# One-hot compares of 512 columns in place of 256 in a recommendation tower on one core

## What is computed

```
e = stack([tbl_f[ids[:, f]] for f in range(32)], axis=1)   # 2048 x 32 x 128
z = einsum('bfd,bgd->bfg', e, e)[:, iu, ju]                # 496 pairs f < g
h = concatenate([z, dense_ctx], axis=1)                    # 2048 x 512
h = maximum(h @ W_top1 + b_top1, 0)                        # 512 -> 512
h = maximum(h @ W_top2 + b_top2, 0)                        # 512 -> 256
y = h @ W_top3                                             # 256 -> 1
```

## Time and profile before

| | us |
|---|---|
| median of the runs | 439.18 |
| runs | 438.72, 439.18, 439.19 |
| the profiled execution's own time | 440.8 |
| its span, first to last instruction | 438.9 |
| TensorE (PE) busy | 396.6 |
| VectorE (DVE) busy | 337.4 |
| GpSimd (POOL) busy | 307.6 |
| ScalarE (ACT) busy | 121.7 |

### The profile page before, as it was taken

The page is one execution under the profiler, slowest core; times in us unless marked ns, Lnnn a source line. Parts: engine busy times, 40 slices in busy tenths (PEclk is TensorE's granted clock), DMA queues, the critical chain, the costliest instruction groups (busy, mean ns, idle before and its releaser), DMA issues.

```text
span 438.9 us, 11697 instructions
## 1 busy us (share of the span) xinstructions
PE 396.6 (90%) x4672; PEld 371.2 (85%) x4672; DVE 337.4 (77%) x873; ACT 121.7 (28%) x220; POOL 307.6 (70%) x324
## 2 busy tenths in 40 slices
PE   0469677999999999999999999999999999999967
PEld 0468577989999889989999989999999999998866
DVE  3789949999498958899498949899589949891510
ACT  1254410133213321233113321233214311332323
POOL 5777877777777777777777777777777777777100
PEclk9998998899999999999999999999999999999999
DMA  6999953435234332424332442436332543332000
GB/s 131 235 240 215 218 174 80 104 78 100 77 83 77 99 98 57 99 75 103 74 81 72 106 93 58 97 79 100 73 86 72 102 93 66 89 74 54 21 3 2
DMA packets 31374, 42.11 MB, mean 96 GB/s; under 512 B 11164, under 2 KB 24220, under 8 KB 31352
## 3 DMA queue, kind: packets, MB, share of 16 engines
q1 hardware_dynamic: 18936, 20.64, 22.7%
q0 software_dynamic: 10240, 20.99, 18.9%
q10 hardware_dynamic: 2176, 0.17, 0.4%
HBM read 41.77 MB, written 0.01 MB: 95 GB/s over the span
## 4 chain that ended last, share of the span: by engine, by line
PE 55%; DVE 28%; issue 6%; DMA 5%; SPq 3%; ACT 1%; DVEq 0%; ACTq 0%
PE sel_ps L295 19%; DVE onehot L628 17%; PE gram_ps L314 12%; PE work_ps L352 11%; DVE pairs L639 9%; PE work_ps L360 6%; DMA pairs<-tables_selected 5%; PE work_ps L277 3%; PE work_ps L425 2%; SPq L227 1%; SPq L222 1%; DVE table_lo L662 1%; PE work_ps L434 1%; PE work_ps L331 1%; DVE pairs L653 1%
## 5 line engine op out<-in xcount | busy, mean ns | idle before, releaser
L248 POOL DMA_INDIRECT gathered<-table,tile_ids x320 | 307.4, 960 | 100.3 <-issue 95.4
L628 DVE TENSOR_SCALAR onehot<-id_rows,row_no 128x256 fp32r<-128x256 int32 x768 | 238.8, 386 | 19.4 <-DMA id_rows<-ids_selected 12.2
L295 PE MATMUL sel_ps<-onehot,table_hi 125*128 125x256 f32 x768 | 202.0, 300 | 30.1 <-DVE table_lo L662 23.1
L295 PE MATMUL sel_ps<-onehot,table_lo 125*128 125x256 f32 x768 | 194.5, 290 | 0.0
L295 PEld LDWEIGHTS sel_ps<-onehot,table_hi 125*128 125x128 f32 x768 | 152.1, 198 | 38.8 <-DVE table_lo L662 24.0
L295 PEld LDWEIGHTS sel_ps<-onehot,table_lo 125*128 125x128 f32 x768 | 152.7, 199 | 0.0
L639 DVE STREAM_TRANSPOSE pairs<-gram_ps 32x1024 f32<-32x1024 f32 x60 | 74.8, 1246 | 56.0 <-PE gram_ps L314 55.3
L487 ACT ACTIVATE rows_T<-sel_ps 128x512 f32<-128x512 f32 x48 | 30.0, 627 | 127.3 <-PE sel_ps L295 91.9
L314 PEld LDWEIGHTS gram_ps<-rows_T 128*64 128x64 f32 x1920 | 57.5, 138 | 7.2 <-issue 7.2
L478 ACT ACTIVATE rows_T<-work_ps 128x512 f32<-128x512 f32 x80 | 45.5, 599 | 61.1 <-PE work_ps L277 61.1
L314 PE MATMUL gram_ps<-rows_T 128*64 128x64 f32 x1920 | 59.6, 223 | 2.4 <-issue 2.4
(11 more groups left out here) (26 smaller groups left out, 84.1 us busy)
## 6 DMA issues: line engine op xcount, KB each, us to landing
id_rows<-ids_selected SPq DMA_DIRECT2D x48, 256.0 KB
gathered<-table,tile_ids POOLq DMA_INDIRECT x320
pairs<-tables_selected SPq DMA_DIRECT2D x6, 448.0 KB
x<-tables_selected SPq DMA_DIRECT2D x6, 448.0 KB
w_sb<-w SPq DMA_DIRECT2D x1, 1024.0 KB
w_sb<-w SPq DMA_DIRECT2D x1, 512.0 KB
pairs<-tables_selected SPq DMA_DIRECT2D x6, 52.0 KB
x<-tables_selected SPq DMA_DIRECT2D x6, 52.0 KB
```

What stands on the lines that cost most here:

```text
L248: nc.gpsimd.indirect_dma_start(gathered[:, t, g, :], None, tables_gathered[g], bass.IndirectOffsetOnAxis(ap=slot_id, axis=0)).then_inc(chu ...
L295: last_op = nc.tensor.matmul(sel_ps[:, u % 2, e, :], part[0:SEL_P, 2 * u + e, k, :], onehot[0:SEL_P, (2 * u + h) % HALF_SLOTS, kk, e, :], ...
L628: last_op = nc.vector.tensor_scalar(onehot[:, (2 * u + h) % HALF_SLOTS, kk, e, :], id_rows[:, slot, e, :], row_no[:, k:k + 1], None, ALU.i ...
```

## The change

From the second pair on one compare makes the one-hots of both features of a unit for one k: 512 columns in place of twice 256. The two features stand side by side in `id_rows` and in `onehot`, so both operands are 512 consecutive elements. The first pair (`known_first`) keeps its compares of 256. Which values are written, the semaphores, the slots and the order of everything else stay.

```diff
--- before.py
+++ after.py
@@ -624,10 +624,16 @@
                         dve.wait_ge(onehot_used, at(i, o, 2 * UNITS, 2 * u + h - HALF_SLOTS + 1))
                     for kk in range(K_HALF):
                         k = h * K_HALF + kk
-                        for e in range(2):
-                            last_op = nc.vector.tensor_scalar(onehot[:, (2 * u + h) % HALF_SLOTS, kk, e, :],
-                                                              id_rows[:, slot, e, :], row_no[:, k:k + 1], None,
-                                                              ALU.is_equal)
+                        hot = onehot[:, (2 * u + h) % HALF_SLOTS, kk, :, :]
+                        if known_first(i, o):
+                            for e in range(2):
+                                last_op = nc.vector.tensor_scalar(hot[:, e, :], id_rows[:, slot, e, :],
+                                                                  row_no[:, k:k + 1], None, ALU.is_equal)
+                        else:
+                            last_op = nc.vector.tensor_scalar(
+                                hot.rearrange("p e s -> p (e s)"),
+                                id_rows[:, slot, :, :].rearrange("p e s -> p (e s)"), row_no[:, k:k + 1], None,
+                                ALU.is_equal)
                     last_op.then_inc(onehot_ready, 1)
```

## The result

| | before | changed |
|---|---|---|
| median of the runs, us | 438.95 (beside it), 439.18 (shown ahead) | 460.06 (457.74 to 460.59) |
| ratio | | 1.0464, 95% interval 1.041 to 1.0518 |
| span of the profiled execution, us | 438.9 | 457.8 (459.7 with what lies around it) |
| VectorE busy, us | 337.4 | 270.9 |
| GpSimd busy, us | 307.6 | 333.4 |

The kernel became 4.6% slower. The sign and the place of the loss are those of the prediction; its size is not: 444.1 was forecast, with 454 as the end of the range.

The account below looks back on a forecast made before the run. GpSimd's gather queue was taken as the bound: 438.9 - 6.9 = 432.0 us, plus 11.8 for delayed gathers, gives a span of 443.8 and a time of 444.1 us. Range 432 to 454, the forecast's own 440 to 449.

Parts of the forecast that it names:

- The queue of gathers without a hole: GpSimd's line: gathers follow each other every 1.25 us, 50.0 us a pair, slower than TensorE's 48.8.
- the 6.9 us in hand: At the last chunk's turn: rows there by 409.6, turned at 416.5; the most a faster VectorE or TensorE can win.
- Two columns at a time: VectorE's compare streams two columns at once, so a 512-column compare takes 394 ns against twice 260.
- 98 were forecast: Gathers met by wide compares: 134 us of comparing on VectorE, at 1.37 us for each met gather.
- the price of one, 0.12 us: Wait of a gather met by wide compares on VectorE: 120 ns each, 11.8 us in all.
- upper bound of 0.21: Highest wait per met gather, 210 ns, if its second access may wait for a stream too; 20.6 us in all.
- Every second one misses the gap: In long rows of wide compares, every second gather waits out nearly a whole stream, 259 ns: 130 on average.
- Rival 3: A gather's second access waits too, 160 to 210 ns each: 448 to 453 us, chance 0.11.
- 4 + 7.3 us: TensorE's gain: 4 us at the second pair's start, 7.3 us of weight-load waits later; TensorE alone would end at 427.6.
- rival 1: Gathers fall in step with longer compares or slip between short rows: up to 30 ns each, 432 to 436 us, chance 0.22.
- rival 4: Doubled compare takes 527 ns so VectorE wins nothing, or gather loss equals the 6.9 us: 438 to 440 us, chance 0.07.
- The small loss by TensorE's clock near the end: TensorE's clock may fall behind waits for gathers near the end: up to 1 us more, inside the range.

Follow-up runs that it names:

- paced: Changed kernel, 512 columns, but each wide compare waits for the end of the one before: 434.83 us, ratio 0.9944 to the kernel before.
- few_256: Kernel before, compares of 256 columns, but from the second pair on only the first feature of each chunk is gathered: 430.67 us, one execution.
- few_512: Changed kernel, compares of 512 columns, but from the second pair on only the first feature of each chunk is gathered: 424.70 us, one execution.
- start_only: Changed kernel with 512-column compares only in the second pair's first units, 256 everywhere else: 436.34 us, ratio 0.9949 to the kernel before.
- the mixture: Kernel before with 512-column compares in the second pair's first units and unit 3's half 1, first-pair subtractions halved: 436.52 us, ratio 0.9946.

## Why the prediction was right or wrong

**Right: what bounds the kernel.** The queue of gathers without a hole and the 6.9 us in hand were the frame of the sum, and it held: in the changed kernel and in paced the span is the last gather's start plus 24.9 us (438.9 - 6.9 - 407.2 = 24.8 in the prediction's numbers), and TensorE's new wait is at L277.

**Right: the compare.** Two columns at a time, 0.48 us, 66.5 us less of VectorE where some 73 were forecast. The earlier trace rows carried this.

**Right: how many gathers are met.** 98 were forecast; 97 took over 1.0 us, and 97 start inside a row of compares. A little luck is in it: the formula divides by the time of a gather that is met, and with the measured price it gives 89.

**Wrong: the price of one, 0.12 us.** That is the term that was mis-sized: 98 gathers at 0.12 us were put at 11.8 us, and the last gather moved by 25.7. A gather that is met lost 25.7 / 97 = 0.26 us (407.2 to 432.9 for the last gather), above the upper bound of 0.21 as well; with 0.26 in its place the sum is 432.0 + 25.7 = 457.7, the span that was measured. Two steps led to it. First, the working took only the first access and let the second be free, since the earlier trace rows showed it free up to 0.7 us into the gather; the traces of the change show that of the second wait only 0.105 us are free. Second, and this is the larger part, the step between the two engines was worked out without the second wait. "Every second one misses the gap" follows from a pitch of 1.25 us. But a gather whose second access has waited is longer: its successor needs its first access 1.34 us after the stream's end at which the wait ended, and not 1.25. Three compares are 1.18 us, so 1.25 would be 0.07 us into the gap of 0.127, and 1.34 is 0.16 us behind a stream's end, in the next stream. In a row without an end every gather would pay 0.34. The rows are short, so only some pay both waits and others the first alone, but none misses the compares, where the prediction let every second one go free. The prediction had looked for a good step, seen that it ends, and put the average of a moving phase in its place. The upper bound was built by adding 80 ns to the same average, and so was no bound. Rival 3 named the second access and stopped at 160 to 210 ns for the same reason.

**Right in direction, too large: TensorE's gain.** 4 + 7.3 us were forecast for TensorE's side alone; the pair few_256 and few_512 shows 6, in one execution each. In the changed kernel this changed nothing, since the gathers end it. The 4 us at the start agree with start_only, whose last turn comes 4.9 us earlier than before (416.51 to 411.56) and even then waits for gathers, though its span is only 3.4 us shorter.

**Not so:** rival 1 (the gathers slip through) and rival 4 (no gain on VectorE). The small loss by TensorE's clock near the end did not occur in the changed kernel: the granted clock is 0.50 from 437.2 to 440.5 us, but the last turn is followed by 22.3 us, against 22.4 before. In start_only and the mixture a fall of the same kind came later and cost 1.6 us.

## What to carry to other kernels

When one engine's queue has no hole, its pace is the floor, however idle its share of busy time looks: multiply count by pitch, and compare the last item with the moment at which it is used. On VectorE fewer and longer instructions are not free for GpSimd's indirect DMAs: before an instruction is widened, count how the two cycles fit into each other, with both accesses. Two periodic engines that exclude each other can keep a good step (0.6 us lost before the change) or a bad one (26.1 behind it), and an average over phases describes neither. Where a long instruction must stay, pacing it took nearly all of the loss away here (`paced`). A shape that takes one column at a time did too, but TensorE then waited for the slower compares (444 us).

## What was not expected of the hardware

A gather and a compare of two columns at a time exclude each other at two moments: 0.05 us after the gather's start, where its wait counts in full, and 0.59 us after that, where the first 0.105 us of waiting are free. Worked out from the changed kernel, these times give most gathers of the runs with 384 and 448 columns within 5 ns as well. They do not hold everywhere: among narrow compares that it does not keep step with, a gather took up to 4.53 us (few_256). A gather also waits for a subtraction with two inputs, up to 1.02 us, and that wait shrinks when the subtraction is cut in two (0.46 us). A compare of 0.73 us that takes one column at a time does not touch it at all. And a compare that waits for its predecessor's end starts only 0.52 us behind the predecessor's start at 512 columns, 0.13 us more than one that does not wait.
